# Weaving four transposes and three products on TensorE in an attention kernel

## The reference

```python
q_hk = (hidden_q @ Wq.T).reshape(b, s, H, K)          # 2 x 512 rows, 16 heads of 128
q_big = jnp.einsum('bshk,hkq->bshq', q_hk, w_kc_q)
kv_rope = kv_c * cos[None] + _rotate_half(kv_c) * sin[None]   # 2 x 1024 rows of 128
q_r = jnp.einsum('bshq,hqr->bhsr', q_big, W_qr)       # 64 wide
k_r = jnp.einsum('bld,hdr->bhlr', kv_rope, W_kr)
scores = jnp.einsum('bhsr,bhlr->bhsl', q_r, k_r)
attn = jax.nn.softmax(scores, axis=-1)
ctx_c = jnp.einsum('bhsl,bld->bhsd', attn, kv_rope)
ctx_lat = jnp.einsum('bhsd,hkd->bshk', ctx_c, w_kc_kv)
out = ctx_lat.reshape(b, s, H * K) @ Wo.T
...
x = x + jnp.tanh(g_xattn[0]) * out
```

## Time and profile before

| | us |
|---|---|
| median of 3 runs | 749.52 (749.51 to 750.24) |
| the profiled execution, its own time | 751.12 |
| its span | 749.3 |
| PE busy in the span | 727.2 (97%) |
| DVE, ACT, POOL busy | 574.7 (77%), 480.6 (64%), 238.8 (32%) |
| mean granted TensorE clock, as a share of full | 0.997 |

### The profile page before, as it was taken

The page is one execution under the profiler, slowest core; times in us unless marked ns, Lnnn a source line. Parts: engine busy times, 40 slices in busy tenths (PEclk is TensorE's granted clock), DMA queues, the critical chain, the costliest instruction groups (busy, mean ns, idle before and its releaser), DMA issues.

```text
span 749.3 us, 11830 instructions
## 1 busy us (share of the span) xinstructions
PE 727.2 (97%) x4080; PEld 519.7 (69%) x4080; DVE 574.7 (77%) x1024; ACT 480.6 (64%) x807; POOL 238.8 (32%) x221
## 2 busy tenths in 40 slices
PE   7899999999999999999999999999999998999997
PEld 6676778676867686778677777777776776654553
DVE  5877877776778677777877787877787899999873
ACT  1666666565566656676666666756675766478876
POOL 5712222122222222222222222222222225576651
PEclk9999999999999999999999999999999999999999
DMA  8301140104010401040114211231121001000001
GB/s 278 134 7 57 34 148 29 58 29 155 28 56 28 154 28 56 28 154 30 56 57 131 81 57 57 90 121 56 31 86 34 2 26 57 1 1 15 29 29 43
DMA packets 21403, 47.83 MB, mean 64 GB/s; under 512 B 3952, under 2 KB 7152, under 8 KB 21232
## 3 DMA queue, kind: packets, MB, share of 16 engines
q1 hardware_dynamic: 20176, 45.49, 18.0%
q10 hardware_dynamic: 1120, 1.77, 0.7%
q0 software_dynamic: 64, 0.00, 0.0%
HBM read 45.16 MB, written 2.10 MB: 63 GB/s over the span
## 4 chain that ended last, share of the span: by engine, by line
PE 82%; DVE 9%; ACT 2%; POOL 2%; issue 2%; DMA 1%; ACTq 0%; POOLq 0%; DVEq 0%
PE ps_b L1276 14%; PE ps_s L1223 13%; PE ps_ctx L1234 9%; PE ps_ctx L1236 7%; PE ps_ctx L1235 7%; PE ps_b L1197 7%; PE ps_s L542 4%; PE ps_b L1146 4%; PE ps_b L1144 4%; PE ps_b L1145 4%; PE ps_b L593 2%; PE ps_b L1176 2%; PE ps_b L1202 2%; PE ps_b L1168 1%; DMA wqr_s<-in_wqr 1%
## 5 line engine op out<-in xcount | busy, mean ns | idle before, releaser
L1077 POOL TENSOR_SCALAR E<-E,small 128x1024 f32<-128x1024 f32 x128 | 148.4, 1160 | 441.4 <-DVE small L1562 441.4
L1372 ACT ACTIVATE et_hi<-ps_b 128x512 fp32r<-128x512 f32 x256 | 153.3, 603 | 186.0 <-PE ps_b L1276 185.9
L1518 DVE TENSOR_TENSOR et_lo<-ps_b,et_hi 128x512 fp32r<-128x512 f32 x256 | 175.7, 686 | 59.6 <-ACT et_hi L1372 57.0
L1557 DVE TENSOR_REDUCE small<-ps_s 128x1 f32<-128x1024 f32 x128 | 155.6, 1217 | 5.9 <-PE ps_s L1223 4.7
L1276 PEld LDWEIGHTS ps_b<-ident,E 128*128 128x128 f32 x1024 | 124.6, 140 | 51.0 <-issue 15.8
L1276 PE MATMUL ps_b<-ident,E 128*128 128x128 f32 x1024 | 154.0, 273 | 2.6 <-DVE q_lo L1518 2.0
L1406 ACT ACTIVATE E<-ps_s,small 128x1024 f32<-128x1024 f32 x128 | 142.9, 1117 | 7.3 <-DVE small L1557 6.8
L1234 PE MATMUL ps_ctx<-et_hi,kv_hi 128*128 128x512 f32 x256 | 120.9, 472 | 0.5 <-DVE ctx_lo L1518 0.5
L1236 PE MATMUL ps_ctx<-et_lo,kv_hi 128*128 128x512 f32 x256 | 101.1, 395 | 0.0
L1235 PE MATMUL ps_ctx<-et_hi,kv_lo 128*128 128x512 f32 x256 | 100.5, 392 | 0.0
L1543 DVE SCALAR_TENSOR_TENSOR x_sb<-ps_b,small,x_sb 128x512 f32<-128x512 f32 x62 | 46.2, 745 | 28.9 <-PE ps_b L1146 28.8
(11 more groups left out here) (174 smaller groups left out, 1009.6 us busy)
## 6 DMA issues: line engine op xcount, KB each, us to landing
w_stage<-in_wffn SPq DMA_DIRECT2D x48, 512.0 KB, 3.4
wo_s<-in_woT SPq DMA_DIRECT2D x8, 512.0 KB, 6.3
wq_s<-in_wq SPq DMA_DIRECT2D x7, 512.0 KB, 6.2
wkcq_s<-in_wkcqT SPq DMA_DIRECT2D x7, 384.0 KB, 4.0
x_sb<-in_x SPq DMA_DIRECT2D x4, 512.0 KB, 6.4
out<-x_sb SPq DMA_DIRECT2D x8, 256.0 KB, 2.0
wqr_s<-in_wqr SPq DMA_DIRECT2D x7, 192.0 KB, 5.2
wkv_s<-in_wkv SPq DMA_DIRECT2D x8, 128.0 KB, 5.6
```

The lines of the kernel that those rows point to most:

```text
L1077: nc.gpsimd.tensor_scalar(e, e, rowinv[:, k:k + 1], 1.0, ALU.mult, ALU.mult).then_inc(scaled, 1)
L1372: return nc.scalar.activation(out, in_, ACT.Copy)
L1518: return nc.vector.tensor_tensor(out, full, hi.bitcast(F32), ALU.subtract)
L1557: nc.vector.tensor_reduce(negmax[:, k:k + 1], ps_s[:, t % 2, :], AX_X, ALU.max, negate=True).then_inc(max_done, 1)
```

## The change

In steps 0, 1, 4, 5 and 6 (those that have products and no scores, `WOVEN_STEPS`) the three products of the first block in `PV_STEP[c]` no longer follow the four turns. They stand between them: turn, product, turn, product, turn, product, turn. `et_done` is still raised by the last turn, and the wait for `et_split` stands ahead of the first product, now behind the first turn. Steps 2, 3 and 7 are as before, and so is the second block of step 5, which follows the woven one. The instructions are the same ones, 4 turns and 3 products.

```diff
+WOVEN_STEPS = tuple(c for c in range(LT) if PV_STEP[c] and c not in SCORE_STEP)
...
+        def pv_matmul(pe, p, w, c, i):
+
+            b = w // 2
+            if i == 0:
+                pe.wait_ge(et_split, 32 * p + (8 * w + c + 1))
+                if c == 0 and not (is0(p) and w == 0):
+                    pe.wait_ge(ctx_done, 4 * p + w)
+            kv, et = ((kv_hi, et_hi), (kv_lo, et_hi), (kv_hi, et_lo))[i]
+            ins = nc.tensor.matmul(ps_ctx[:, :], kv[:, b, c, :], et[:, c % ET_RING, :], start=(c == 0 and i == 0),
+                                   stop=(c == LT - 1 and i == 2))
+            if i == 2:
+                ins.then_inc(pv_done, 1)
+
         def pv_matmuls(pe, p, w, c):
...
+            for i in range(3):
+                pv_matmul(pe, p, w, c, i)
...
+                    woven = None
+                    if c in WOVEN_STEPS and not (variant == "first" and w < PV_STEP[c][0][0]):
+                        back, tile = PV_STEP[c][0]
+                        woven = ((p, w - back) if w >= back else (p - 1, 3)) + (tile,)
                     for s in range(ST):
                         last = nc.tensor.transpose(into[:, s * P:(s + 1) * P],
                                                    E[:, w % 2, s, c * P:(c + 1) * P], ident[:, :])
-                    last.then_inc(et_done, 1)
+                        if s == ST - 1:
+                            last.then_inc(et_done, 1)
+                        elif woven:
+                            pv_matmul(pe, *woven, s)
...
-                    for back, tile in PV_STEP[c]:
+                    for back, tile in PV_STEP[c][1 if woven else 0:]:
```

More of the change, by code:

```diff
@@ L1226, in score_matmuls @@
                             last.then_inc(scores_done, 1)
-        def pv_matmuls(pe, p, w, c):
[L1230 to L1237, removed]
+        def pv_matmul(pe, p, w, c, i):
[9 more added lines that the diff above has]
+                ins.then_inc(pv_done, 1)
+        def pv_matmuls(pe, p, w, c):
+            for i in range(3):
+                pv_matmul(pe, p, w, c, i)
         def wait_bank(pe, p, variant, user):
```

## The result

| | us |
|---|---|
| before, median of 4 runs beside it | 749.79 (749.51 to 750.24) |
| after, median of 4 runs | 770.87 (769.47 to 771.88) |
| after / before | 1.0272, 95% interval 1.0254 to 1.0289 |
| profiled execution after: its own time, its span | 771.88, 770.1 |
| mean granted TensorE clock after, share of full | 0.998 |

The change makes the kernel 21.1 us slower. 765 was predicted, within 756 to 777. The span grew by 770.1 - 749.3 = 20.8 us, and the mean clock did not move. A part of the scatter between executions of one kernel, some 2 us, comes with the granted clock near their start; what that does to these numbers stands under "What the sum left out".

What follows compares the result with a forecast made beforehand. TensorE's own work was taken as the bound. Added waits of 4.8 + 4.8 + 2.3 + 1.4 + 1.0 + 1.5 = 15.8 us on the 749.3 us span, carried to the median, gave 765 us, range 756 to 777.

Steps and rivals of the forecast that it cites:

- rival 3: Each change between turn and product on TensorE itself costs 10 to 80 ns, up to 25 us on top; chance 12%.
- The change on TensorE itself: nothing.: A woven block of 4 turns and 3 products takes 1.13 us on TensorE, as before.
- the 80 ns: First product behind a turn shows 472 ns, the second 392; as a true cost, 25 us over 158 woven steps.
- The end of the turns.: The last turn, and with it et_done and ScalarE's copy, comes 0.69 us later in each of 158 woven steps.
- (a): Task q in step 2 of unit 1, pairs 0 to 6, waits 0.69 us longer each: 4.8 us.
- (b): Turns of step 2 in unit 2, pairs 0 to 6, wait 0.69 us longer through k_lo: 4.8 us.
- (c): First turn of a unit: 0.69 us slack used up, about 0.11 us lost at 21 boundaries, 2.3 us.
- (e): Task a in step 2 of unit 0, pairs 1 to 6, waits for copies into mz: 0.16 us each, 1.0 us.
- (d): Two boundaries of pair 0 where GpSimd ends last get the whole delay through steps 4 and 5: 1.4 us.
- (f): Pair 7's scores in step 3 wait for the second exponential: two at 0.69 us, one at 0.15, 1.5 us.
- Rival 1: Idle time of ScalarE and VectorE covers the delay, so no difference, 749.5 us; chance 6%.
- Rival 2: Turns hide beside products on TensorE, saving 0.155 us per woven step; net 8 us faster, 741; chance 6%.

Runs made afterwards that it cites:

- e5: Changed kernel with the three products put ahead of the four turns in the 158 steps, nothing alternating: 770.43 us, ratio 1.0281.
- e2: Changed kernel with only step 0 woven (31 of 158 woven steps): 762.72 us, ratio 1.0168.
- e6: Changed kernel with one product between the third and fourth turn and two behind: 753.72 us, ratio 1.0052.
- e7: Changed kernel with TensorE's hardware loop over pairs 1 to 3 written out: 769.65 us, ratio 1.0269.
- e4: Changed kernel with only step 6 woven (32 of 158 woven steps): 757.12 us, ratio 1.0090.
- e1: Changed kernel with only steps 4 and 5 woven (64 of 158 woven steps): 752.83 us, ratio 1.0028.
- e8: Kernel before the change with TensorE's hardware loop over pairs 1 to 3 written out: 750.17 us, ratio 1.0011.
- e10: Kernel before the change with block 5's products moved from step 7 to the next unit's step 0, only at units 1 and 2: 748.79 us, ratio 0.9982.

## Why the prediction was right

The mechanism held at nearly every place, and the size came out short: 15.8 us were summed, and the change itself brought 18.66 in the middle part and 1.30 behind it, 20.0. The measured 770.9 lies at the upper edge of the 757 to 771 given for the likeliest case alone. The range reached to 777 on account of rival 3, which the runs refute.

**The change on TensorE itself: nothing.** Right within 1 to 2 us: a woven step is 0.01 us longer (step 3 to step 7, against e5). Over the 30 stretches from step 3 to step 7 the differences add up to 1.0 us; at that rate all 158 woven steps are an estimated 1.8. Both bounds of 24 and 25 us were far off, and so was the 80 ns on which rivals 2 and 3 leaned.

**The end of the turns.** 0.69 us later was right: 1.03 us from first to last turn, 1.34 to ScalarE's copy.

**(a) and (b)** came out at 0.70 us for each of the 14 places, 9.8 us against 9.6, and e2 shows them alone. Step 0 is their source.

**(c)** cost 0.12 to 0.14 us in written-out code, 0.11 predicted, and e6 shows the slack: 0.23 of delay costs nothing there. In the loop of pairs 1 to 3 it cost 0.25. **(e)** is 0.30 - 0.13 = 0.17 us in pairs 5 and 6, 0.16 predicted, but 0.36 in the loop. The loop's excess over the prediction is (0.34 + 0.14 + 0.14) x 3 = 1.8 us, and e7 took 1.7 away. At pair 4 neither (c) nor (e) showed: 0.27 less. There two small matmuls and four short VectorE instructions for the mean of the weights (348.48 to 349.29 before) stand at the start of unit 0. They come ahead of VectorE's two maxima, which run without a gap up to `mz` before and after, so a late `et_hi` finds VectorE busy.

**(d)** was right in size (1.36 and 1.37), but the cause I gave for the second boundary is not borne out: steps 4 and 5 alone gave 0.08 there, and step 6 alone (e4) 0.68. The delay of this boundary comes by the turns of step 6; that the size fitted was luck.

**(f)** is 0.80 + 0.69 + 0.30 less twice 0.11 for (c): 1.57 against 1.5.

**What the sum left out** is the loop (1.8), alternation (1.0), and the end of the run (1.30, where I had written that unit 3 is covered; e1 shows that it isn't in pair 7). Together 15.8 - 0.27 + 1.8 + 1.0 + 1.3 = 19.6 us, against the 20.0 that were added behind the first scores. The other 0.84 of the span stands ahead of them, where no step is woven. TensorE's rows near the start, before:

```profile
10.85 2.33 PE L1168 MATMUL ps_b<-wqr_s,wkcq_s 128*128 128x128 f32 x12 [2.92 <-DMA wqr_s<-in_wqr]
```

and after:

```profile
11.51 2.52 PE L1169 MATMUL ps_b<-wqr_s,wkcq_s 128*128 128x128 f32 x12 [3.35 <-DMA wqr_s<-in_wqr]
```

A load of weights came 0.66 us later in this execution. Behind this wait both executions were granted half the clock for a while: 0.50 from 12 to 14 us, the lower of its two levels (1.2 and 2.4 GHz). From 48 us to 619 it was 1.00 in both. In the traces of e4 to e6 and e8 to e10 it was 1.00 at the start too, TensorE had idled 1.44 to 2.66 us for the same load, and the first scores begin at 46.2 to 46.8 us. In the seven traces where the clock fell it had idled 2.92 to 3.35, and they begin at 48.0 to 48.9. So some 2 us between two executions lie in the start, whatever the order of the turns. By the spans behind the first scores the change costs 20.0 us, and the 21.1 of the medians holds some of that scatter.

**The signs that were named.** The waits grew as said (`q` 0.24 to 0.95, `k_lo` 0.36 to 7.3 / 7 = 1.04). "Some 20" more first turns behind GpSimd are 11 more in the table of waits: where GpSimd ends nearly with the work ahead, the table names another releaser, as `et_lo` for the load at 280.21, where GpSimd's scaling ended only at 280.09. In e7, with the loop written out, it names GpSimd 22 times, 20 more than before. TensorE's idle time grew by 13.6 us and its busy time by 7.2, not by 15 and 0. Most of that is no dearer work, for e5, with unbroken turns, has 732.4 us busy, 5.2 more than before. The end of a matmul is modelled, and a stall counts as idle only from there, so each new stall hides its first part: before `q` the load rows show 6.6 us of waiting after the change, the matmul rows 4.9. The other 2.0 are near the estimate of 1.8 for the alternation.

**The rivals.** Rival 1 holds where slack is (units 0 and 3 in e6, most starts in e1), and not at the 18 waits. Rival 2 is out: turns don't hide beside products, and the pitch of 0.345 us from turn to turn is the plain sum. The Trainium skill, TensorE: Matmul & The Clock Gate, Part 3 (The mechanism), lets weight loads be pulled ahead of matmuls in flight where the row groups don't conflict or the load goes to the background weight buffer. The timeline after agrees that a load runs ahead, but in it the load of a product begins with the turn ahead of it (both at 316.77), one place ahead and no more. Rival 3 is 1 to 2 us and not 25.

## What to carry to other kernels

Rearranging equal work on the bounding engine does not come free just because the sum of its pitches stays the same: ask when the last instruction that raises a semaphore now ends, and follow that lateness down the lists of the other engines to the next place where the bounding engine waits for them. A place that waits already pays all of it, a place with slack pays only what exceeds the slack, and two late chains into one wait cost the larger and not the sum. The same reading finds gains: where such a wait stands, move work of the bounding engine that nobody needs yet ahead of it, and only there.

## What the runs showed of the hardware

- Transposes of 128 by 128 in fp32 and products of 512 columns, one by one between each other, run at 0.345 us a pair (the mean of 139 woven steps in the trace after), against 0.34 from the neighbours of the order before: 0.01 us for a step of three.
- TensorE's hardware loop costs nothing while TensorE isn't newly held up (e8: the middle part is 0.07 us longer without it), but 0.1 to 0.3 us at each start of a unit 0, 2 or 3 where the late turns hold it up (e7), and nothing at unit 1, where it waits for `q` before and after.
- After 2.92 and 3.35 us in which TensorE idled for a DMA, the granted clock was 0.50 from 12 to 14 us; after 2.43 us in e8 it stayed at 1.00. The same 12 instructions on `wqr_s` took 2.33 and 2.52 us against 1.60.
